# A graph network on one Trainium2 core: edge rows gathered once in aligned blocks, attention reading them linearly

## The reference, cut to what matters

```python
x = (node_inp @ W).reshape(N, H, D)                 # one W for each of R = 4 relations; H = 8, D = 16
es, ed = einsum('nhd,hd->nh', x, a_s), einsum('nhd,hd->nh', x, a_d)
logit = where(mask, leaky_relu(es[src] + ed[dst], 0.2), -1e30)
p = exp(logit - segment_max(logit, dst)[dst]) * mask
out = segment_sum(p / segment_sum(p, dst)[dst] * x[src], dst)
...
msg = leaky_relu(concat([nf[src2], nf[dst2], ef2]) @ We1) @ We2      # second layer
red = segment_sum(msg, dst2)
```

## Time and profile before

| | before |
|---|---|
| median of 3 runs | 6374.5 us (6373.39 to 6383.16) |
| profiled execution, first to last instruction | 7540.9 us |
| setup and schedule, to 30 us; node inputs, to 177 us | 30 and 147 us |
| relation maxima, 177 to 2011 us | 1834 us |
| relation attention, 2011 to 3865 us | 1854 us |
| node update and mix, 3865 to 4190 us | 325 us |
| inputs of layer two, messages, outputs | 110, 3095 and 146 us |
| busy: PE, VectorE, ScalarE, POOL | 61%, 55%, 19%, 58% |
| mean granted TensorE clock | 0.736 |

### The profile page before, as it was taken

How to read it: one execution, slowest core, us unless ns; L and a number is a source line. 1 busy time by engine, 2 the same in 40 slices (tenths; PEclk the granted TensorE clock), 3 DMA queues, 4 the chain that set the end, 5 groups by cost and what they waited for, 6 DMA issues and landing times. The chain is left out here.

```text
span 7540.9 us, 122469 instructions
## 1 busy us (share of the span) xinstructions
PE 4592.3 (61%) x23458; PEld 3407.9 (45%) x23458; DVE 4140.2 (55%) x14519; ACT 1449.7 (19%) x3676; POOL 4394.5 (58%) x3871
## 2 busy tenths in 40 slices
PE   5333333333367777777736577777777777777776
PEld 3232222222356566656625254444544444454445
DVE  4343333334555555555578565565656655565654
ACT  2000000000132332323333311111111111111111
POOL 0554444544344445444452188888888888888871
PEclk9555555555577767677766788888888888888888
DMA  4110000001211112121242488888878888878874
GB/s 124 5 4 4 4 4 4 4 4 4 25 43 43 44 43 45 43 44 44 43 90 46 142 175 169 170 168 167 170 167 169 169 169 168 168 167 169 169 160 120
DMA packets 791940, 691.67 MB, mean 92 GB/s; under 512 B 381442, under 2 KB 646658, under 8 KB 791892
## 3 DMA queue, kind: packets, MB, share of 16 engines
q0 software_dynamic: 267296, 433.63, 31.1%
q1 hardware_dynamic: 524596, 257.53, 13.7%
HBM read 515.53 MB, written 175.11 MB: 92 GB/s over the span
## 5 line engine op out<-in xcount | busy, mean ns | idle before, releaser
L1392 POOL DMA_INDIRECT sums<-msg_bsum,msg_sidx x928 | 1548.4, 1669 | 313.2 <-issue 282.3
L547 POOL DMA_INDIRECT max_es<-esrc,max_idx x928 | 894.2, 964 | 1035.7 <-DVE max_lastloc L590 761.6
L769 POOL DMA_INDIRECT att_xg<-xrel,att_idx x928 | 879.9, 948 | 1025.1 <-DVE att_px L827 682.9
L1534 PEld LDWEIGHTS msg_fwd_ps<-msg_onehot,msg_hid 128*128 128x128 f32 x3712 | 636.4, 224 | 1395.4 <-issue 1295.0
L1401 POOL DMA_INDIRECT msg_ga<-ab,msg_idx x928 | 953.3, 1027 | 392.3 <-issue 240.2
L1547 PE MATMUL msg_pre_ps<-msg_rw,msg_lt 128*128 128x512 f32 x1856 | 1122.8, 691 | 57.5 <-issue 31.8
L1534 PE MATMUL msg_fwd_ps<-msg_onehot,msg_hid 128*128 128x64 f32 x3712 | 627.1, 299 | 765.7 <-DVE l_fwd L1453 464.2
L928 PE MATMUL att_sum_ps<-att_px,att_keyhot 128*128 128x136 f32 x3712 | 786.5, 375 | 214.4 <-issue 95.5
L1505 ACT ACTIVATE msg_bsum<-msg_bwd_ps 128x256 f32<-128x256 f32 x928 | 354.8, 383 | 2561.6 <-PE msg_bwd_ps L1536 1832.7
L928 PEld LDWEIGHTS att_sum_ps<-att_px,att_keyhot 128*128 128x128 f32 x3712 | 680.4, 264 | 334.9 <-DVE l_acc L835 178.2
L702 PE MATMUL max_runT_ps<-k_ident,max_run 32*128 32x32 f32 x928 | 114.1, 280 | 1137.4 <-DVE max_run L619 1040.3
(11 more groups left out here) (228 smaller groups left out, 7476.8 us busy)
## 6 DMA issues: line engine op xcount, KB each, us to landing
msg_rw<-ab SPq DMA_DIRECT2D x928, 128.0 KB
msg_lt<-in_efT SPq DMA_DIRECT2D x928, 32.0 KB
max_rec<-in_rec SPq DMA_DIRECT2D x928, 3.0 KB
max_es<-esrc,max_idx POOLq DMA_INDIRECT x928
att_edw<-edm SPq DMA_DIRECT2D x928, 16.0 KB
att_xg<-xrel,att_idx POOLq DMA_INDIRECT x928
msg_ga<-ab,msg_idx POOLq DMA_INDIRECT x928
sums<-msg_bsum,msg_sidx POOLq DMA_INDIRECT x928
```

The lines of the kernel that those rows point to most:

```text
L547: pool.indirect_dma_start(es[:, b, u, :], None, T.esrc, bass.IndirectOffsetOnAxis(ap=idx[:, b % 2, u:u + 1], axis=0)).then_inc(s_es[b], 16)
L769: pool.indirect_dma_start(xg[:, b, u, :], None, T.xrel, bass.IndirectOffsetOnAxis(ap=idx[:, b, u:u + 1], axis=0)).then_inc(s_xg[b], 16)
L1392: pool.indirect_dma_start(T.sums[u % 2], bass.IndirectOffsetOnAxis(ap=sidx[:, b, u:u + 1], axis=0), bsum[:, b, u, :], None, compute_op=ALU ...
L1534: pe.matmul(fwd_ps[u % 2][:, q * WIN:(q + 1) * WIN], hid[:, b % 2, u, HID + q * P:HID + (q + 1) * P], onehot[:, b, u, :], start=True, stop ...
```

## The change

`schedule` becomes `lists`. Edges are now cut into 832 aligned blocks of 128 (NB), whatever their destinations. A step is a pair of a block and a window that touches it, so a block on a border is read by both windows, with a test that drops foreign edges. There are two step lists: windows of 64 nodes for layer two (STEPS, again 928) and windows of 32 nodes for the attention (KSTEPS, 1028). `lists` loads all records at once, counts where each node's edges end with 52 counting passes over the block heads, 52 indirect loads of blocks, and 50 passes each for the position and the presence of a node, then gathers the blocks of both step lists (17 indirect loads).

`relation_maxima` gathers whole rows of 576 bytes (16 products and a one for each head, then the 8 source terms), one indirect transfer a block, 104 groups of 8. SP stores them in DRAM in edge order (`xe`), and the scan of each block (`run`). The window parts of the old stage are gone. The new `node_maxima` gathers each node's last scan row with 50 indirect transfers and lays the maxima out by key in SBUF (`K.edm`).

`relation_attention` has no gather: SP loads a block's rows linearly and a row of keys. A key is relation times 32 plus node, so a step has 128 keys, the expansion is one matmul of 16 columns that picks relation and node at once, and a step needs one matmul of sums instead of two. POOL makes the one-hot `keyhot`. The turning of the one-hot and the mask work are gone. There are 257 groups of 4.

```diff
-XR = C + H
-STEPS = -(-((N_EDGES + (P - 1) * WINDOWS) // P) // (2 * G)) * (2 * G)
+HW = D + 1
+XR = H * HW
+XW = XR + H
+KWIN = 32
+U4 = 4
+NB = -(-(BLOCKS + 1) // G) * G
+STEPS = -(-(BLOCKS + WINDOWS - 1) // U4) * U4
+KSTEPS = -(-(BLOCKS + KWINDOWS - 1) // U4) * U4
...
+            for c in range(THR):
+                if c in (0, 2):
+                    pool.wait_ge(s_made, AT_NODES if c else AT_PAIRS)
+                    settle(pool, K)
+                pool.indirect_dma_start(dst[:, c, :], None, T.dst,
+                                        bass.IndirectOffsetOnAxis(ap=block_i[:, c:c + 1], axis=0)).then_inc(s_get, 16)
...
+            def store_rows(j, b):
+                sp.wait_ge(s_xe[b], filled(j, b, RG, 16 * G))
+                settle(sp, K)
+                sp.dma_start(xrows[ds(j, 1), :, :, :].rearrange("j e u c -> (j e) u c"), xe[:, b, :, :]).then_inc(s_xst[b], 16)
...
-                    pool.indirect_dma_start(es[:, b, u, :], None, T.esrc,
-                                            bass.IndirectOffsetOnAxis(ap=idx[:, b % 2, u:u + 1], axis=0)).then_inc(s_es[b], 16)
+                    pool.indirect_dma_start(xe[:, b, u, :], None, T.rows,
+                                            bass.IndirectOffsetOnAxis(ap=idx[:, b, u:u + 1], axis=0)).then_inc(s_xe[b], 16)
...
-                    sp.dma_start(edw[:, b, u, :], T.edm[ds(w[u] * WIN, WIN), :]).then_inc(s_ed[b], 16)
+                sp.dma_start(keyrow[:, b, :], key[ds(j, 1), :].to_broadcast([P, U * P])).then_inc(s_kr[b], 16)
+                for u in range(U):
+                    sp.dma_start(xe[:, b, u, :], T.xe[ds(e[u], P), :]).then_inc(s_xe[b], 16)
...
-                    pool.indirect_dma_start(xg[:, b, u, :], None, T.xrel,
-                                            bass.IndirectOffsetOnAxis(ap=idx[:, b, u:u + 1], axis=0)).then_inc(s_xg[b], 16)
+                    pool.tensor_scalar(keyhot[:, b, u, :], K.ramp[:, 1:P + 1], keys[:, b, u:u + 1], None,
+                                       ALU.is_equal).then_inc(s_kh, 1)
...
+            def tick(t, h, has):
+                slot = lambda skew: (h - skew) % RG
+                if has(4):
+                    w = windows.of(t - 4, slot(4))
+                for u in range(U):
+                    if has(4):
+                        add(t - 4, slot(4), u, w[u])
+                    if has(2) and u < 3:
+                        select(t - 2, slot(2), u)
+                    if has(3) and u == 2:
+                        weigh(t - 3, slot(3))
+                if has(1):
+                    spread(t - 1, slot(1))
...
-            pipeline(pe, GROUPS, RG, [(4, sums), (1, expand), (0, transpose)])
+            pipeline(pe, GROUPS, RG, [(3, sums), (1, expand)])
```

More of the change, by code:

```diff
@@ L42 @@
 EPS = 1e-5
-REC = 6
 def flat(ap):
@@ L259, in schedule @@
[L259 to L264, removed]
-        block = ph.block()
+        thr = ph.sb("thr", [P, THR])
+        thr0 = ph.sb("thr0", [P, TILES])
+        part32 = ph.sb("part32", [P, 1])
+        blocks = ph.sb("blocks", [P, THR])
@@ new lines, in lists @@
+        off_ps = ph.ps("off_ps", [P, 2 * P])
+        tp_ps = [ph.ps(f"tp_ps{b}", [P, 4, P]) for b in range(4)]
+        s_first, s_rec, s_made, s_get, s_row, s_st, s_off, s_tp, s_cp = (
+            ph.sem(x) for x in ("first", "rec", "made", "get", "row", "st", "off", "tp", "cp"))
+        AT_PAIRS, BEGIN, INDEX, AT_NODES, DIAG, STEPLIST, KEY, LOC = range(1, 9)
+        block = ph.block()
+        by_group = lambda t: t[:, :].rearrange("e (j u) -> e u j", u=G)
+        by_step = lambda t, kc: t[:, :].rearrange("e (s k) -> e k s", k=kc)
@@ L267, in _ @@
+        for k in range(0, KC, 4):
+            moves.append((4, [step[:, v, 0, :] for v in range(k, k + 4)], by_step(K.src, KC)[:, k:k + 4, :], P))
+        for k in range(0, KC, 4):
+            moves.append((6, [loc[:, v, :] for v in range(k, k + 4)], by_step(K.loc, KC)[:, k:k + 4, :], P))
         @block.sync
@@ L281, in _ @@
         @block.tensor
         def _(pe):
[L283 to L291, removed]
+            pe.wait_ge(s_made, DIAG)
@@ new lines, in _ @@
+            pe.matmul(off_ps[:, :], K.ones[:, :], flat(diag[:, :, :]), start=True, stop=True).then_inc(s_off, 1)
+            for g, (kind, ins, out, n) in enumerate(moves):
+                if kind == 1:
+                    pe.wait_ge(s_row, 3)
+                elif kind == 2:
+                    pe.wait_ge(s_made, INDEX)
+                elif kind == 4:
+                    pe.wait_ge(s_get, 16 * (THR + KKC + KC))
+                elif kind == 5:
+                    pe.wait_ge(s_made, KEY)
+                else:
+                    pe.wait_ge(s_made, LOC)
+                if g >= 4:
+                    pe.wait_ge(s_cp, g - 3)
+                for u, a in enumerate(ins):
+                    last = pe.transpose(tp_ps[g % 4][:, u, 0:n], a, K.ident[0:n, 0:n])
+                last.then_inc(s_tp, 1)
@@ L293, in _ @@
+        @block.scalar
+        def _(act):
+            act.wait_ge(s_rec, 16)
+            act.activation(rows[:, :, 0, :], rec[:, :, 0].rearrange("j (u e) -> j u e", u=G), ACT.Copy).then_inc(s_row, 1)
+            for g, (kind, ins, out, n) in enumerate(moves):
+                act.wait_ge(s_tp, g + 1)
+                act.activation(out, tp_ps[g % 4][:, 0:len(ins), 0:n], ACT.Copy).then_inc(s_cp, 1)
         @block.vector
@@ L390, in _ @@
             L, M = Links(dve, s_v), K.setup.on(dve)
+            for b in range(2):
+                M.mark(dve.memset(heads(rows[:, b, :, 0:XR])[:, :, :, D:HW], 1.0))
             dve.wait_ge(s_w, 80)
@@ L910, in expand @@
[L910 to L917 removed]
+            windows = Windows(nc, pe, mybir.EngineType.PE, K.reg_kw, KWINDOWS - 1, U, RG, 1)
```

832 lines of the change are left out of this document (406 added, 426 removed).

## The result

| | before | after |
|---|---|---|
| median of 4 runs each | 6376.5 us (6373.39 to 6383.16) | 6691.1 us (6688.0 to 6696.01) |
| ratio | | 1.0492, 95% interval 1.0477 to 1.0507 |
| profiled execution | 7540.9 us | 6686.9 us |
| mean granted TensorE clock | 0.736 | 0.708 |

The change costs 315 us; 301 were forecast. The clock of 0.736 is that of the long profiled execution of before; in other executions of that kernel, which took 6367 to 6386 us, it was 0.78 to 0.80. The profiled execution of after agrees with its timed runs, so its stages can be read directly. Here is its table of stretches, the counterpart of the earlier trace rows (start:end, length; PE, PEld, DVE, ACT, POOL busy; clock, DMA share, GB/s): lists, node inputs, maxima, node maxima, attention, update and mix, inputs of layer two, messages, outputs.

The account below looks back on a forecast made before the run. It took POOL to bound the messages, and a new ring through TensorE and VectorE to bound the changed attention. 220 - 10 - 176 + 96 + 186 - 15 = +301 us on 6374.5 gave 6675 us, range 6340 to 6830.

Parts of the forecast that it names:

- setup and lists: Setup stage: serial chain of load, counts, indirect loads and passes takes 250 us instead of 30, +220 us.
- node inputs: Node inputs stage: rows grow by 6%, two small matmuls a tile and one store go, -10 us.
- maxima and node maxima: Maxima at 1063 us against 1239, -176; new node maxima stage with 50 gathers and passes, +96.
- attention: Attention: 257 groups at 5.6 us a turn plus 30, 1469 us against 1283, +186 us.
- update to end: Update and mix lose the store and load of `valid`, -15 us; messages unchanged.
- rival D: Maxima: new stores of rows hold the gathers back; at 12 us a group +208, 6883 us; chance 0.05.
- I take a mean between them, about 0.6: Attention's TensorE clock, taken between 0.71 (attention before) and 0.55 (maxima), giving 5.6 us a turn.
- Rival A: Attention: the clock stays up because pauses are short; 4.3 us a turn, 6380 us, no change; chance 0.15.
- the ring: Attention: product, sums, expansion, `logit`, next product wait in turn; 6.1 us at the lower clock, 4.3 at the higher.
- Rival B: Attention: the ring doesn't bind, SP's issue decides at 4.0 us a turn; 6265 us; chance 0.12.
- Rival C: Attention: VectorE and POOL get in each other's way, 0.47 us a turn, 120 us more, 6795 us; chance 0.13.

Follow-up runs that it names:

- e7_before_half: Kernel before with its attention run over the first 116 of 232 groups: 5744.1 us beside 6377.3.
- e12_wide5: Changed kernel plus five 512-column matmuls a turn that nobody reads, behind the expansion: 6405.3 us, 1.0044 of before.
- e1_ahead: Changed kernel, ring opened: expansion issued ahead of the sums, its key comparison at the turn's top, SP's key-row load not waiting for the product: 6149.0 us.
- e5_filler: Changed kernel plus fourteen 128-column matmuls that nobody reads behind each expansion: 6685.9 us.
- e3_expand_twice: Changed kernel with each of the four expansion matmuls of a group issued twice: 7132.0 us.
- e9_pool_one_column: Changed kernel with POOL comparing one column of 128 of each attention one-hot, selection by key left out: 6688.8 us.
- e14_shared: e1_ahead plus four 512-column matmuls a turn, each group's fourth comparison moved from POOL to VectorE: 6286.5 us where before took 7318.2.

## Why the prediction was right, and where it was off

The stages of before are taken from `e7_before_half`, whose profile is undisturbed, those of after from its own. Its first `node_h` started at 71.1, its first gather at 186.9, its first `logit` at 1446.5, the update at 2065.9 us; after has 272.3, 368.6, 1525.3 and 3014.3. The half attention of 619.4 us and the 633.2 us that it saved make 1252.6 us for the whole.

| term | forecast | measured |
|---|---|---|
| setup and lists | +220 | 272.3 - 71.1 = +201 |
| node inputs | -10 | 96.3 - 115.8 = -20 |
| maxima and node maxima | -176 + 96 = -80 | 1156.7 - 1259.6 = -103 |
| attention | +186 | 1489.0 - 1252.6 = +236 |
| update to end | -15 | 3672.6 - 3676.1 = -4 |
| sum | +301 | +312 (timed: +315) |

- **Setup.** Right in kind. A counting pass is 1.08 us, as the earlier trace rows had it (52 of them, 56.1 us), and the next starts 1.12 us after it, where 1.28 were assumed; POOL's loads waited for them as said.
- **Maxima.** A group takes (1421.0 - 368.6) / 103.9 = 10.1 us, 10.0 forecast; a row of 576 bytes costs POOL a median of 944 ns, as one of 32 did; the stores hold nothing back, so rival D falls. Node maxima took 85 us, not 96.
- **Attention.** The mechanism was the forecast's: `logit` behind the expansion, the expansion behind the sums, the sums behind the product. Its sizes were off twice, in opposite directions. The parts at the lower clock are sums 2.0 us (2.0 forecast), expansion 1.7 (2.0), `logit` to the product's end 1.8 (1.9), signalling 0.3 (0.2): 5.8 us where the forecast's own sum has 6.1. And the clock was 0.50 throughout, where it says "I take a mean between them, about 0.6", and so 5.6 us. At 0.50 its sum would have given 6.1 us a turn and 1598 us, 102 above the 1496 measured (1518.4 to 3014.3); the clock taken too high brought it to 1469. So it is partly luck that 5.6 us came near 5.78. Of the 50 us by which this row of the table misses, 27 are the new stage (1496 against 1469) and 23 the old one, which was shorter than assumed (1260 against 1283).
- **The sum.** It came near the timed result because setup and maxima were 42 us better than said, about as much as the attention was worse. That is luck as well.
- **Rival A** (the clock stays up, 6380 us) is not what happened, but it was priced well: `e12_wide5`, where the clock comes up to 0.82, took 6405 us. By the rule of the Trainium skill that the prediction cited ("TensorE: Matmul & The Clock Gate", oscillation), pauses as short as the 2 us of the ring should have left the clock up. In after that was not put to the test: the clock was 0.50 already when the stage began, so what was missing is a rise, and it was missing in `e1_ahead` too, which has no pauses. Where it was up and fell, the trace does not agree with the rule: `e5_filler` has 0.78 in its first 31 us and 0.50 from 1600 us on, with TensorE shown busy for 44.6 of 50 us. The prediction's own reading that the clock "stays raised" in the earlier trace rows goes no further than the row: in the next 10.2 us of that trace it is 0.50 again.
- **Rival B** (the ring doesn't bind) falls with `e3_expand_twice`, and its price for SP, 3.9 us a turn from the earlier trace rows, was too high: a load of after occupies SP's queue for 0.47 us (four in 1.88), not 0.77.
- **Rival C** falls with `e9_pool_one_column`. The Trainium skill ("SBUF — State Buffer", two separate sides) speaks of an exclusive lock between the two engines; the rows show a small price on both sides, 604 to 729 ns for POOL's comparison and 184 to 249 ns for `leaky`, each in time that was to spare. Single comparisons took up to 1219 ns in `e1_ahead`, so POOL may well have waited for a whole product now and then; that VectorE ever waited for a whole comparison is not to be seen.

## What to carry to other kernels

When an edit shortens the distance between a producer and its user in a hand-written order, walk the ring through both engines before adding up busy times: here every engine had at least a third of its time free and the stage still got slower, and three small moves, made together, in the written order were worth 542 us. Before a cost is read from a profile whose span differs from the timed runs, find out which stretches carry the excess, and compare the rest. And when TensorE's work is thinned out, reckon with the clock as a term of its own: look at the granted clock of the stage before, and price the turn at the lower level too.

## What the runs showed that was not expected

- The granted clock did not go by how full TensorE was shown. It was 0.50 with 937 of 944 us busy (`e1_ahead`) and with 1318 of 1484 (`e5_filler`), but 0.87 in the attention before with 527 of 626 us. Five 512-column matmuls a turn, work that nobody reads, took it to 0.99 in the opened ring and to 0.82 in the ring as written: 83 and 286 us gained.
- The standstills of the earlier trace rows are not a trait of one execution. On one occasion all seven runs of the kernel before took about 7318 us, 941 more than elsewhere, which is near the 7540.9 us of the profile that the prediction started from. The kernels of that occasion had them in the maxima, where POOL gathers, and hardly at all in an attention without gathers. What brings them about, and what after itself would take there, was not tried. An estimate for after: its 6691 us and the 189 by which the maxima of `e14_shared` were longer make about 6880 us, below the 7318 of before. So the comparison with before may well come out the other way there.
- Gathering costs POOL by the transfer, not by the byte, over the range seen here: 944 ns (median) for rows of 32, 544 and 576 bytes.
